# Attention weights transposed by VectorE in 32x32 squares instead of by TensorE, with the graphs laid on their tokens' partitions

## The reference

```python
adj = dep_type_matrix != 0
dep_emb = dep_emb_table[dep_type_matrix]
hi_t = einsum('bid,de->bie', h, W1_w[:HID])[:, :, None, :] + einsum('bijd,de->bije', dep_emb, W1_w[HID:]) + W1_b
hj_t = einsum('bjd,de->bje', h, W2_w[:HID])[:, None, :, :] + einsum('bijd,de->bije', dep_emb, W2_w[HID:]) + W2_b
relevance = sum(hi_t * hj_t, axis=-1)
A = softmax(where(adj, relevance, NEG), axis=2)
h_syn = relu(einsum('bij,bjd->bid', A, h) @ gcn_w + gcn_b)
x = layernorm(x + h_syn @ Wo_w + Wo_b)
```

## Time and profile before

| | |
|---|---|
| median of 3 runs | 378.48 us (378.05 to 378.74) |
| span of the profiled execution, first to last instruction | 377.4 us |
| the median over that span (what lies around it) | 1.08 us |
| TensorE busy | 369.0 us, 98% of the span |
| VectorE, ScalarE, GpSimd busy | 245.0, 198.5 and 145.0 us |
| mean granted TensorE clock | 0.997 of full speed |

### The profile page before, as it was taken

The page is one execution under the profiler, slowest core; times in us unless marked ns, Lnnn a source line. Parts: engine busy times, 40 slices in busy tenths (PEclk is TensorE's granted clock), DMA queues, the critical chain, the costliest instruction groups (busy, mean ns, idle before and its releaser), DMA issues.

```text
span 377.4 us, 9989 instructions
## 1 busy us (share of the span) xinstructions
PE 369.0 (98%) x3859; PEld 320.1 (85%) x3859; DVE 245.0 (65%) x693; ACT 198.5 (53%) x437; POOL 145.0 (38%) x108
## 2 busy tenths in 40 slices
PE   8998999999999999999999999999999999999994
PEld 5786898988989898898989889898988989888893
DVE  1556568485765847577584757748475774847756
ACT  1576837356283735718264471826447282635562
POOL 1504552617053271705417160441716144141814
PEclk9999999999999999999999999999999999999998
DMA  7994206465342645525254552625545262550033
GB/s 226 344 328 131 77 6 214 131 180 173 91 173 83 201 146 173 174 80 185 83 187 161 171 163 76 202 83 181 167 146 169 79 217 83 168 168 3 2 126 128
DMA packets 43268, 55.48 MB, mean 147 GB/s; under 512 B 10352, under 2 KB 37488, under 8 KB 43248
## 3 DMA queue, kind: packets, MB, share of 16 engines
q1 hardware_dynamic: 42448, 54.30, 45.4%
q10 hardware_dynamic: 800, 0.90, 0.7%
HBM read 42.61 MB, written 12.58 MB: 146 GB/s over the span
## 4 chain that ended last, share of the span: by engine, by line
PE 94%; ACT 2%; DMA 2%; DVE 1%; issue 0%; POOL 0%
PE banks L462 26%; PE banks L464 25%; PE banks L463 25%; PE banks L529 7%; PE banks L483 6%; PE banks L569 2%; DMA xt_sb<-in_x_t_dram 2%; PE banks L558 1%; PE banks L510 1%; ACT less_sb L798 1%; DVE z_lo L952 1%; ACT xt_hi L795 0%; ACT prob L773 0%; PE banks L579 0%; DVE rel L970 0%
## 5 line engine op out<-in xcount | busy, mean ns | idle before, releaser
L871 DVE TENSOR_TENSOR y_sb<-banks,y_sb 128x384 f32<-128x384 f32 x60 | 33.4, 557 | 77.3 <-PE banks L464 77.3
L1144 POOL TENSOR_TENSOR y_sb<-y_sb,wob_sb 128x1536 f32<-128x1536 f32 x15 | 52.9, 3527 | 62.5 <-DVE y_sb L893 49.4
L785 ACT CAST z_hi<-banks 128x512 fp32r<-128x512 f32 x48 | 26.6, 589 | 83.2 <-PE banks L529 77.9
L462 PE MATMUL banks<-wo_hi,hs_hi 128*128 128x384 f32 x180 | 60.5, 336 | 0.0
L463 PE MATMUL banks<-wo_lo,hs_hi 128*128 128x384 f32 x180 | 60.5, 336 | 0.0
L464 PE MATMUL banks<-wo_hi,hs_lo 128*128 128x384 f32 x180 | 60.5, 336 | 0.0
L462 PE MATMUL banks<-xt_hi,m_hi 128*128 128x512 f32 x144 | 58.4, 406 | 0.0
L462 PE MATMUL banks<-z_hi,gcn_hi 128*128 128x512 f32 x144 | 58.0, 402 | 0.0
L464 PE MATMUL banks<-z_hi,gcn_lo 128*128 128x512 f32 x144 | 56.6, 393 | 0.0
L464 PE MATMUL banks<-xt_hi,m_lo 128*128 128x512 f32 x144 | 56.5, 392 | 0.0
L463 PE MATMUL banks<-z_lo,gcn_hi 128*128 128x512 f32 x144 | 56.3, 391 | 0.0
(11 more groups left out here) (108 smaller groups left out, 616.4 us busy)
## 6 DMA issues: line engine op xcount, KB each, us to landing
x_sb<-in_x_dram SPq DMA_DIRECT2D x16, 768.0 KB, 4.6
xt_sb<-in_x_t_dram SPq DMA_DIRECT2D x15, 768.0 KB, 6.6
y_sb<-in_x_dram SPq DMA_DIRECT2D x15, 768.0 KB, 4.6
out_dram<-y_sb SPq DMA_DIRECT2D x30, 384.0 KB, 2.5
adj_sb<-in_adj_dram SPq DMA_DIRECT2D x32, 64.0 KB, 3.1
xt_sb<-in_x_t_dram SPq DMA_DIRECT2D x2, 384.0 KB, 6.8
xt_sb<-in_x_dram SPq DMA_DIRECT2D x1, 768.0 KB, 6.1
w2t_sb<-in_w_t_dram SPq DMA_DIRECT2D x3, 192.0 KB, 4.6
```

The source lines that it names most:

```text
L462: pe.matmul(acc, a_hi, b_hi, start=first, stop=False)
L785: act.copy(by_graph(z_hi[:, f, :]), mixed(f)).then_inc(zhi, 1)
L871: dve.tensor_tensor(y_home(g, slot)[:, q, :], out_bank(g, q)[:, 0:HID], y_home(g, slot)[:, q, :], ALU.add).then_inc(added, 1)
L1144: pool.tensor_tensor(y_home(g, slot), y_home(g, slot), wob_sb[:].rearrange("p (o n) -> p o n", o=1).to_broadcast([P, PAIRS, HID]), ALU.add ...
```

## The change

VectorE makes the transpose. One instruction transposes every 32x32 square of `weights` in place into `at_sb`, and four further instructions, of 32 partitions by 4 x 32 columns each, put the off-diagonal squares of each 64x64 graph where they belong. They stand in VectorE's queue directly after `weights`. TensorE's `turn`, its semaphore and ScalarE's copy are gone. The adjacency of a group is loaded so that each graph lies on the partition half where its tokens lie; score and mix follow that order, `turned(q)` is gone, and the row terms become one instruction. In group 0 the third x split leaves ScalarE's queue; it is done whole in group 1, between the row terms and the exponentials. The diff, cut to its core:

```diff
 P = 128
+SQUARE = 32
 NEG = 1.0e9
...
     xt_cols = x_t.rearrange("(c p) (g t) -> g p c t", p=P, t=GT)
-    adj_rows = adj.rearrange("(g e n) i j -> g e i n j", e=2, n=PAIRS)
+    adj_rows = adj.rearrange("(g n e) i j -> g e i n j", e=2, n=PAIRS)
...
         normed = sem("normed")
-        turn_mm = sem("turn_mm")
+        turned = sem("turned")
         at_ready = sem("at_ready")
...
                         for e in range(2):
-                            q, h = HALVES * e + n // 2, n % 2
-                            ts = slice(q * P + h * NODES, q * P + (h + 1) * NODES)
+                            ts = slice(n * P + e * NODES, n * P + (e + 1) * NODES)
                             mm = pe.matmul(score[e * NODES:(e + 1) * NODES, n * NODES:(n + 1) * NODES],
...
-            def turned(q):
-
-                at = q % HALVES * P + q // HALVES * NODES
-                return slice(at, at + NODES)
-
-            def turn(g):
-                pe.wait_ge(normed, 2 * (g + 1))
-                for v in range(HALVES):
-                    mm = pe.transpose(score[:, v * P:(v + 1) * P],
-                                      weights[:, 2 * v:2 * v + 2, :].rearrange("p h n -> p (h n)"), ident[:])
-                mm.then_inc(turn_mm, 1)
-
             def mix(g, par):
...
                                     x_sb[rows, par, q, f * P + e * NODES:f * P + (e + 1) * NODES],
-                                    at_sb[rows, turned(q)], start=True, stop=True)
+                                    at_sb[rows, q * NODES:(q + 1) * NODES], start=True, stop=True)
                     return mm
...
                 if static(g, 0):
-                    proj(1, 1, PROJ1_BANK, range(2, C * C - 1))
-                    pe.wait_ge(ident_ready, 1)
-                    turn(g)
-                    proj(1, 1, PROJ1_BANK, range(C * C - 1, C * C))
+                    proj(1, 1, PROJ1_BANK, range(2, C * C))
                     return
...
                 gemm(g - 1)
-                turn(g)
                 if static(g, LAST):
...
                 act.wait_ge(xu_ready, g + 1)
-                for e in range(2):
-                    for h in range(2):
-                        at, of = slice(e * NODES, (e + 1) * NODES), slice(h * NODES, (h + 1) * NODES)
-                        a = act.activation(srow[at, h:PAIRS:2], xu_row[of, HALVES * e:HALVES * (e + 1)], ACT.Identity,
-                                           bias=k_sb[of, 0:1])
-                a.then_inc(srow_ready, 1)
+                act.activation(srow[:], xu_row[:], ACT.Identity, bias=k_sb[:, 0:1]).then_inc(srow_ready, 1)
...
                     weigh(g)
-                    project_out(1, PROJ1_BANK, range(1, 2))
-                    act.wait_ge(xt_loaded[par], 32)
-                    act.copy(xt_hi[:, par, 0], xt_sb[:, par, 0])
-                    act.wait_ge(turn_mm, 1)
-                    act.copy(at_sb[:], score[:, 0:MIX]).then_inc(at_ready, 1)
-                    act.copy(xt_hi[:, par, 1], xt_sb[:, par, 1])
-                    project_out(1, PROJ1_BANK, range(2, C))
-                    act.copy(xt_hi[:, par, 2], xt_sb[:, par, 2]).then_inc(xhi, 1)
+                    project_out(1, PROJ1_BANK, range(1, C))
                     return
...
                     row_terms(g)
+                    split_x(g + 1, 1 - par)
                 weigh(g)
                 hidden(g - 1)
-                act.wait_ge(turn_mm, g + 1)
-                act.copy(at_sb[:], score[:, 0:MIX]).then_inc(at_ready, 1)
                 if before(g, LAST - 1):
...
                                          less_sb[:, f, :], ALU.max, ALU.subtract).then_inc(hslo, 1)
+
+            def turn(g):
+
+                dve.wait_ge(normed, 2 * (g + 1))
+                dve.transpose(at_sb[:], weights[:].rearrange("p q n -> p (q n)")).then_inc(turned, 1)
+                dve.wait_ge(turned, g + 1)
+                crossed = at_sb[:].rearrange("p (q n) -> p q n", n=NODES)
+                for to, of in ((1, 0), (0, 1), (3, 2), (2, 3)):
+                    i, j = of % 2 * SQUARE, to % 2 * SQUARE
+                    a = dve.transpose(crossed[to * SQUARE:(to + 1) * SQUARE, :, i:i + SQUARE],
+                                      weights[of * SQUARE:(of + 1) * SQUARE, :, j:j + SQUARE])
+                a.then_inc(at_ready, 1)
...
                                   .to_broadcast([P, PAIRS, NODES]), ALU.mult).then_inc(normed, 1)
+                turn(g)
                 if static(g, LAST):
```

## The result

The changed kernel takes 376.85 us (median of 5 runs, 376.19 to 377.10), the kernel before 378.48 us: a ratio of 0.9943, 95% interval 0.9927 to 0.9960. It is faster, by 0.6% and not by 1.2%; the forecast was 373.9 us, and 376.85 lies above the range that ended at 376.0. The profiled execution of the changed kernel took 376.19 us at a span of 374.3 us.

A forecast was written before the change was run, and what follows sets the result against it. TensorE was taken to bound the kernel, busy 369.0 of 377.4 us. Gains of 3.0 (its transposes), 1.2 (start) and 0.43 us (last group) made 4.6, so 378.48 became 373.9 us; range 372.9 to 376.0.

The forecast's parts named there:

- Part 1: Two TensorE transposes between gemm and projection: removing them gains 0.21 us per group, 14 x 0.21 = 3.0 us.
- Parts 2 and 3: Steady groups: the five VectorE transposes cost nothing while under 2.30 us; ScalarE's saved copy and row terms gain nothing.
- T: Time of the five VectorE transposes: 1.64 us taken, 1.35 low, 2.2 high.
- the cover: Steady group: how long VectorE's transposes may last before the output product waits for the hidden layer's low halves, 2.30 us.
- "Middle" to "High": Estimates for the five VectorE transposes: 1.64 us to 2.2 us, the latter with each small one as dear as the big.
- Part 5: Last group: no TensorE transposes (0.21 us) and no wait of mix 15 for ScalarE's copy (0.22), a gain of 0.43 us.
- Part 4: Start: masking 0.72 us sooner, mix 0 at 30.1, 1.2 us sooner; moved x split at no cost, 0.6 us to spare.
- The little and the far pass of the cover: Rivals: transposes outlast VectorE's spare time in steady groups; a little gives 376.8 us, chance 0.08; far gives 399, chance 0.07.
- The transposes were not free on TensorE: Rival denied here: TensorE's transposes were hidden in weight loads, so only start and last-group gains remain, 377.1 us; chance 0.03.
- "later x split": Rival: ScalarE or GpSimd 1 us later holds projection 2, 374.3 us, or 375.0 with the start's gain lost; chance 0.06.

The follow-up runs named there:

- run 6: Changed kernel with two unread TensorE transposes put back behind gemm in groups 1 to 15, VectorE's transposes kept: 379.46 us, ratio 1.0004.
- run 10: Changed kernel with each of the four small VectorE transposes done a second time into an unread array: 388.06 us, ratio 1.0243.
- Run 4: Changed kernel with the third x split back at the end of group 0 on ScalarE's queue: 375.77 us, ratio 0.9921.
- run 2: Changed kernel with group 1's running maximum over the adjacency moved behind its row products: 376.00 us, ratio 0.9926.
- the third trace: The kernel before, unchanged, traced once more for the scatter of its start: 378.78 us, span 377.0 us.
- run 9: Changed kernel with four row-term instructions put back in place of the one: 377.71 us, ratio 0.9961.

## Why the prediction was half right

**Right: the steady groups.** Part 1 gave 0.21 us for the two transposes; 13 groups gave 2.91 us, 0.22 each, and run 6 took it back. Parts 2 and 3 held as well: T is 1.77 us against 1.64 (0.445 for the large transpose, 0.303 for a small one, 1.25 for four), and neither VectorE nor ScalarE makes a steady group wait. The Trainium skill, "VectorE: DVE Perf Modes", section "Two Vector instructions with no wait between them", by which an instruction that starts in another quadrant than the one before it is held until the earlier ones are done, agrees with the trace: four times 0.31 us with no overlap, and in run 10 an overlap only inside a pair on one quadrant. The signs named for "right" came: 0.23 us between gemm and projection, 21.92 us per group, and no wait for the low halves in the steady groups. One sign named for "wrong" came too, once: the output product waiting for VectorE, in the last group.

**A size off in Part 2: the cover.** It was given as 2.30 us; run 10 puts it at 2.12. The sum left out the 0.06 us from VectorE's end to TensorE's start, and an overlap that is lost: before, the first row product began at 171.93, 0.09 us ahead of the end of the weights, and now it begins at 171.56, 0.03 behind the last transpose. In run 10 a wait also cost 0.12 us more than it lasted, 0.10 of it in the matmul behind it. With T = 1.77 this does no harm, but "Middle" to "High" was not all without a stall: by these numbers T = 2.2 would have cost 13 x (0.08 + 0.12) = 2.6 us, an estimate.

**Wrong, 1.40 us: Part 5.** "0.43 us" counted mix 15 alone. The prediction checked what the transposes delay in a steady group and did not repeat the check for the last one, where VectorE's and TensorE's orders differ: the output product of group 13's last pair waits for the first low half of hidden layer 14 already, and that now stands behind 1.77 us of transposes. The cover there was 0.27 us, not 2.30. Measured: a loss of 0.97 instead of a gain of 0.43. Run 1 takes the low half ahead of the transposes (and the final maximum out of its way) and has the forecast gain.

**Wrong, 0.71 us: the moved x split in Part 4.** "No cost" rested on a cover of 0.6 us towards projection 2, which held: the split ends 8.6 us after mix 0, where 8.8 was forecast, and projection 2 starts at 39.08, 9.4 us after it, with no wait. "GpSimd has nothing else to do then", said against the rival, was true too. What was not asked is what VectorE does beside GpSimd: its maximum reads two arrays from SBUF, was stretched from 0.42 to 3.29 us, and ended with GpSimd's split. The loss then went on by VectorE's queue to the row products, to `wo_lo` and to TensorE. Run 4 (no GpSimd beside it) removes the loss; run 2 (the maximum elsewhere) removes 0.5 us of it, since the weights then meet the split. The Trainium skill, "SBUF — State Buffer", section "Who interferes with whom", says that a VectorE instruction with two SBUF inputs contends with a GpSimd instruction that reads SBUF, and that whoever comes first keeps the shared port to its end. The trace agrees: with the split issued first, the maximum is done 0.29 us after it (38.28 and 38.57); the mask addition that VectorE had begun 0.05 us earlier keeps its 0.42 us, and the split is then 0.25 us longer (3.75). The prediction had a small case of this in its own rows. The row product of 0.74 us at the start reads two arrays from SBUF, and it began at 29.40 while GpSimd's mask was at work:

```profile
29.16 0.58 POOL L1137 TENSOR_SCALAR neg_sb<-adj_sb 128x256 f32<-128x256 int32 x1 [9.97 <-DVE weights L989]
```

It was booked as "something beside VectorE's work", 0.2 us, and its cause was not looked for. In the third trace the two meet in the same way (the mask at 28.82 for 0.58 us, the row product at 29.06 for 0.74); in the changed kernel nothing on VectorE that reads two arrays from SBUF runs beside the mask there, and it takes 0.41 us.

**Wrong, 0.80 us: the start in Part 4.** The side after the change was right: 30.1 - 22.72 = 7.38 us from score 0 to mix 0 were forecast, 7.50 measured. The side before it was read from one execution in which the output weights (`wo_sb`) had landed late. "Masking starts ... 0.72 sooner" is true of that execution; in the third trace masking starts 1.72 us after score 0 with four row terms, against 1.67 with one, and run 9 finds 0.14 us. The 0.2 us added to the transposes was not needed: they end 1.77 us after the weights at the start too, beside the same mask (0.41 us), and mix 0 follows 0.15 us later. That 1.64 + 0.2 came close to these 1.92 us is luck. What is left of the start's gain on the third trace is 0.40 us, 0.35 of it between the masking and mix 0, where ScalarE's copy and what it waited for are gone.

The three errors and the 0.18 us that the steady groups gave more make 1.40 + 0.71 + 0.80 - 0.18 = 2.73 us; the terms of the forecast, 4.57 us (14 x 0.21 is 2.94, which it rounded to 3.0), less this are the 1.84 us of the table. **What lies around the span** was also mis-sized: 1.08 us was the median less the span of an execution that was itself longer (377.4 us) than the typical one (377.0). In every timed run it is 1.8 to 1.9 us. Since the sum was made on the median, this moved nothing by itself; but it was a sign, not read, that the traced execution was not the median one, and a gain read from it was taken off the median.

**The rivals.** The little and the far pass of the cover did not come; run 10 shows the mechanism they named, at T above 2.12. The transposes were not free on TensorE. The "later x split" was the right edit, but it held VectorE and not projection 2; its second time has a slip, 374.3 and the lost 1.2 us make 375.5, not 375.0, which changes no chance. What stays open is the scatter of score 0's start, and how often an execution of the kernel before has the late transfer: its timed runs reach from 378.1 to 381.3 us, and only three of its executions were traced.

## What to carry to other kernels

When work is put into an engine's queue, follow every wait behind it in each group that is written out on its own, the last one above all: the cover of the loop's body does not hold there. Before an instruction is moved "where the engine is idle", look at what the other engines run beside it, and at VectorE instructions with two SBUF inputs beside GpSimd first; moving one of them away can hand the collision to the next (run 2). A gain at the start of a kernel is read from more than one execution, since the landing of a transfer decides what it is worth.

## What the hardware showed that was not expected

- GpSimd's elementwise work stops a VectorE instruction with two SBUF inputs almost to its end: 3.29 and 3.57 us instead of 0.42 for the maximum, 1.43 for the weights (run 2), each done 0.28 or 0.29 us after GpSimd. The reduction that makes the row maximum (0.42 us) and instructions with one input from PSUM beside the split, and the transposes beside the mask, kept their times.
- In one execution of the kernel before (run 5), TensorE's clock fell to 0.50 after two waits of 1.15 and 1.03 us, and mix 0 to mix 1 became 1.4 us longer. What sets the fall off is open: in the trace the prediction rests on, TensorE waited 0.47 and 1.07 us at the same places and was busy for 1.11 of the 2.48 us ahead of mix 0, as in run 5, and in run 10 it waited 1.8 us there at one stretch; both times the clock stayed at 1.00. Of the 45 executions of the kernel before that were timed with runs 1 to 12, seven took over 380 us, at a mean granted clock of 0.991 to 0.993; the others had 0.995 or more.
- Transposes of 32 partitions by 128 numbers on VectorE: 0.303 us each on changing quarters, 0.26 us and 0.07 us of overlap when the quarters are those of the one before.
